# Edge net of a graph kernel: a visit's mask by six comparisons of a row with a column each

## The chip, the cores and the metric

One NeuronCore of a Trainium2 chip. The metric is the time of one execution on the device in microseconds, the median of three. A profile is one further execution, taken by the hardware profiler.

## The reference

6250 nodes with 64 features and 200,000 edges with a source and a destination (sorted by destination, denser towards low nodes) go through four layers of a graph network; each is preceded by a layer norm and a relu, and its result is added to `x`. The change lies in the last layer:

```python
src, dst = (edge_index[0], edge_index[1])
x = jnp.concatenate([node_features[src], node_features[dst], edge_features], axis=-1)
h = jax.nn.relu(x @ W1.T + b1)
messages = h @ W2.T + b2
agg = jax.ops.segment_sum(messages, dst, num_segments=node_features.shape[0])
...
return (1.0 - z) * n + z * node_features
```

## The kernel before

The three other layers multiply by a dense matrix of edge counts and are not touched. The last layer has a relu per edge, so it must go over every edge; this stage is called the edge net.

Edges lie in chunks of 128, one edge on each partition; six chunks are a group (GC = 6), 261 groups in all. Nodes lie in 49 tiles of 128. Since edges are sorted, a group holds edges of one tile or of neighbouring ones. A *visit* is a pair of group and tile; there are 309 (NV). Low tiles have many groups, high ones few, so that towards the end about three groups make four visits.

**GpSimd** fetches the source side. For each group it issues six indirect gathers (L704, one per chunk), each from `ptable` in DRAM (a row of 64 fp32 per node) into a slot of `grow`, a ring of eight groups in SBUF. The addresses are a column of `src_i` in SBUF. It does nothing else here. **SyncE** (`group`, L563 its wait) hands the slots on: it waits until the visits of the group four before are done, frees a slot, waits until the rows of this group have landed and counts up `s_land`, on which VectorE waits.

**ScalarE** issues two plain transfers per visit (`edge_rows`): the low bits of the destinations, broadcast to all partitions (`dst_rows`), and the edge features. It also computes the relu (L907).

**TensorE**, for a visit: `new(t, m)` makes the destination side with a one-hot matrix (L959) and adds the edge features' product (L962), into PSUM, two visits ahead. `seg(m)` (L970) sums messages by node: six matmuls, chunk j's mask as weights, against the three bf16 parts of its messages.

**VectorE**, for a visit, in program order (`visit`, one loop body unrolled for four visits, at whose head it loads the registers of the four; `m` is the slot of four):
- it waits for TensorE (`s_z`) and for the gathered rows (`s_land`)
- L1383: adds part 0 in PSUM to the gathered rows, 384 elements per partition
- L1346 `mask` of the next visit: 1 where edge and node of the tile agree, 128 x 6 elements
- L1383: adds part 1
- L1350 `relative`: six destinations less the tile's first node, for the visit after next
- L1383: adds part 2; ScalarE's relu starts
- L1357 `turned`: the one-hot matrix of the visit after next, by one comparison of 768 bf16 elements with a column
- it waits for the relu; L1406: its residual after one bf16 part; L1362: sums TensorE's result of two visits before; L1412: the second residual; L1367: adds the sum into `pair`.

The mask before compares `drel`, six int16 numbers per partition, each broadcast over 128 nodes, with `itiles`, a constant table of node numbers in [node][chunk] order. So a visit's masks are stored with the chunk innermost, and the weights of one chunk are read with a stride of six elements.

Of the kernel before, what the change touches and what calls it, by code (L numbers as in the profile page):

```python
# [22 lines left out]
P = 128  # L23
N = 6250
E = 200000
H = 64
# [9 lines left out]
GC = 6  # L36
# [5 lines left out]
DEEP = 4  # L42
# [37 lines left out]
bf16 = mybir.dt.bfloat16  # L80
# [5 lines left out]
ALU = mybir.AluOpType  # L86
ACT = mybir.ActivationFunctionType
AX = mybir.AxisListType.X
ds = bass.ds


def gnn(nc, D, out):
    with ExitStack() as ctx:
        def sb(name, shape, dt=f32):
            return ctx.enter_context(nc.sbuf_tensor(name, shape, dt))
# [46 lines left out]
        dst_s = sb("dst_s", [P, CHP], i16)  # L142
# [9 lines left out]
        iota_h = sb("iota_h", [P, WC], f16)  # L152
# [3 lines left out]
        tbase = sb("tbase", [P, NTP])  # L156
# [15 lines left out]
        stat_w = sb("stat_w", [P, 2 * NW])  # L172
# [12 lines left out]
        idx_at = itile_at + P // 2  # L185
# [7 lines left out]
        itiles = sb("itiles", [P, P, SC], i16)  # L193
# [52 lines left out]
        def late_part(width):  # L246
            lp[0] += width
            assert lp[0] <= 2 * CHP
            return late[:, lp[0] - width:lp[0]]
# [24 lines left out]
        def net_part():  # L274
            net_used[0] += DEEP * GC * P // 2
            assert net_used[0] <= TC
            return arena[:, net_used[0] - DEEP * GC * P // 2:net_used[0]]

        masks = net_part().bitcast(bf16).rearrange("p (q d j) -> p q d j", q=DEEP, j=GC)
        onehotT = net_part().bitcast(bf16).rearrange("p (q e) -> p q e", q=DEEP)  # L280
        dst_rows = net_part().bitcast(bf16).rearrange("p (q e) -> p q e", q=DEEP)
        e32t = net_part()[0:2 * F32, :].rearrange("p (q e) -> p q e", q=DEEP)
        drel = sb("drel", [P, 4, GC], i16)
        gath_w = late_part(GC * 3 * H // 2)
        gath = parts3(gath_w)
        qblk = gath_w[:, 0:TB * H].rearrange("p (n f) -> p n f", f=H)
# [631 lines left out]
        def _(pe):  # L918
# [33 lines left out]
            def edge_net():  # L952

                def new(t, m):
                    z = (ps_front, ps_back)[m % 2]
                    pe.wait_ge(s_ohT, 1)
                    pe.sem_inc(s_ohT, -1)  # L957
                    for j in range(GC):
                        pe.matmul(z[:, j // 2, j % 2 * 3 * H:(j % 2 + 1) * 3 * H], onehotT[:, m, j * P:(j + 1) * P],  # L959
                                  qsp[:, ds(t, 1), :], start=j % 2 == 0, stop=False)  # L960
                    for b in range(TH):
                        last = pe.matmul(edge_z[m % 2][:, b, :, 0, :], e32t[:, m, b * P:(b + 1) * P],  # L962
                                         W["w_e3"][:, :].rearrange("p (c f) -> p c f", f=H), start=False, stop=True)
                    last.then_inc(s_z, 1)

                def seg(m):
                    pe.wait_ge(s_rl, 1)
                    pe.sem_inc(s_rl, -1)  # L968
                    for j in range(GC):
                        last = pe.matmul(ps_d[:, m % 2, 0:3 * H], masks[:, m, :, j], msg_h[:, m, j, :, :],  # L970
                                         start=j == 0, stop=j == GC - 1)
                    last.then_inc(s_sg, 1)

                def visit(n, m, t):
                    if n is None or n + 2 < NV:
                        new(t, (m + 2) % DEEP)
                    seg(m)

                new(0, 0)
                t1 = pe.value_load(visit_tab[0:1, 0:1, 3, 3:4].rearrange("o b w -> o (b w)"), min_val=0, max_val=NT - 1)  # L980
                new(t1, 1)
                all_visits(pe, 2, 3, visit)
# [289 lines left out]
        def _(v):  # L1272
            def link(ins):

                ins.then_inc(s_v, 1)
                v.wait_ge(s_v, 1)
                v.sem_inc(s_v, -1)
# [65 lines left out]
            def edge_net():  # L1343

                def mask(m, n2):
                    return v.tensor_tensor(masks[:, m, :, :], drel[:, n2, :].unsqueeze(1).broadcast_to([P, P, GC]),  # L1346
                                           itiles[:, :, :], ALU.is_equal)

                def relative(c, t, n2):
                    return v.tensor_scalar(drel[:, n2, :], dst_s[:, ds(c, GC)], tbase[:, ds(t, 1)], None, ALU.subtract)  # L1350

                def turned(m):
                    v.wait_ge(s_db[m], 16)
                    v.sem_inc(s_db[m], -16)
                    v.wait_ge(s_et[m], 16)
                    v.sem_inc(s_et[m], -16)
                    v.tensor_scalar(onehotT[:, m, :], dst_rows[:, m, :], pcol[:, 0:1], None, ALU.is_equal).then_inc(s_ohT, 1)  # L1357

                def summed(m):
                    v.wait_ge(s_sg, 1)  # L1360
                    v.sem_inc(s_sg, -1)
                    return v.tensor_reduce(red[:, m % 2, :], ps_d[:, m % 2, 0:3 * H].rearrange("p (k f) -> p f k", k=3),  # L1362
                                           AX, ALU.add)

                def total(t, m):
                    sums = pair[:, ds(t, 1), 0:H].rearrange("p t f -> p (t f)")
                    return v.tensor_tensor(sums, sums, red[:, m % 2, :], ALU.add)  # L1367

                def visit(n, m, g1, c2, t2, before):

                    def has(k):
                        return n is None or 0 <= n + k < NV

                    q = nc.s_assert_within(v.snap((g1 + (RING - 1)) % RING), 0, RING - 1,
                                           skip_runtime_bounds_check_because="the remainder of a group's number")
                    v.wait_ge(s_z, 1)
                    v.sem_inc(s_z, -1)
                    v.wait_ge(s_land, v.snap(g1 & 511))
                    z = edge_z[m % 2]
                    sums = msg[:, m, :, 2, :].rearrange("p (b c) f -> p b c f", c=2)  # L1380

                    def add(k, other):
                        return v.tensor_tensor(sums, z[:, :, :, k, :], other, ALU.add)  # L1383

                    def linked(links):
                        v.wait_ge(s_v, links)
                        v.sem_inc(s_v, -links)

                    links = 1 if has(-3) else 0
                    add(0, grow[:, ds(q, 1), :, :].rearrange("p r (b c) f -> p (r b) c f", c=2)).then_inc(s_v, 1)  # L1390
                    if has(1):
                        mask((m + 1) % DEEP, (m + 1) % 2)
                    linked(1 + links)
                    add(1, sums).then_inc(s_v, 1)
                    links = 0
                    if has(2):
                        relative(c2, t2, m % 2).then_inc(s_v, 1)
                        links += 1
                    linked(1 + links)
                    add(2, sums).then_inc(s_y, 1)  # L1400
                    if has(2):
                        turned((m + 2) % DEEP)
                    v.wait_ge(s_r1, 1)
                    v.sem_inc(s_r1, -1)  # L1404
                    v.sem_inc(s_done, 1)
                    v.tensor_tensor(msg[:, m, :, 1, :], msg[:, m, :, 0, :], msg_h[:, m, :, 0, :], ALU.subtract).then_inc(s_v, 1)  # L1406
                    links = 1
                    if has(-2):
                        summed(m).then_inc(s_v, 1)
                        links += 1  # L1410
                    linked(links)
                    v.tensor_tensor(msg[:, m, :, 2, :], msg[:, m, :, 1, :], msg_h[:, m, :, 1, :], ALU.subtract).then_inc(s_rl, 1)  # L1412
                    if has(-2):
                        total(before, m).then_inc(s_v, 1)

                v.memset(pair[:, :, 0:H], 0.0)
                t1 = v.value_load(visit_tab[0:1, 0:1, 3, 3:4].rearrange("o b w -> o (b w)"), min_val=0, max_val=NT - 1)
                c1 = v.value_load(visit_tab[0:1, 0:1, 3, 0:1].rearrange("o b w -> o (b w)"), min_val=0, max_val=PAD_C)
                link(v.tensor_copy(drel[:, 0, :], dst_s[:, 0:GC]))
                mask(0, 0)  # L1420
                link(relative(c1, t1, 1))
                for m in range(2):
                    turned(m)
                all_visits(v, 0, 4, visit)
                v.wait_ge(s_v, 1)
                v.sem_inc(s_v, -1)
                for k in (NV - 2, NV - 1):
                    before = visits(v, (k + 2) // 4, 0, 4)[(k + 2) % 4][3]
                    link(summed(k))
                    link(total(before, k))  # L1430
# [608 lines left out]
```

## Time and profile before

| | |
|---|---|
| time, median of 3 | 4882.58 us (4882.41 to 4883.76) |
| the profiled execution | 4881.64 us, its span 4879.8 us |
| mean granted TensorE clock | 0.707 of full speed over the span, 0.50 in the edge net |
| edge net, from the first gather to the last sum | 2769.9 to 4787 us |
| busy over the span | TensorE 3312.7, VectorE 2846.7, ScalarE 886.2, GpSimd 2046.2 us |

Busy times of the span are averages over stages that have different limits; for the change, the edge net's own rows count. In them a start is in us from the span's start, the duration in us follows, and a bracket names what ended the idle time before.

### The profile page before, as it was taken

How to read it: one execution, taken by the hardware profiler on the slowest of the kernel's cores; microseconds unless marked ns; L12 is line 12 of the kernel's file. 1: busy time of each engine (PE TensorE's matmuls, PEld its weight loads, DVE VectorE, ACT ScalarE, POOL GpSimd, SP SyncE). 2: the span in 40 equal slices, each digit the busy share in tenths (PEclk: the TensorE clock that was granted, in tenths of full speed). 3: DMA queues.
4: the chain of work that ended last, by engine and by line, in shares of the span. 5: the costliest groups of instructions: out<-in, count | busy, mean ns of one | idle time of the engine just before them, and what ended most of it. 6: DMA issues, size and time to landing. Idle time of an engine off the chain costs nothing. (4 is left out here: it accounts for less than half of the span.)

```text
span 4879.8 us, 93316 instructions
## 1 busy us (share of the span) xinstructions
PE 3312.7 (68%) x24444; PEld 2509.9 (51%) x24445; DVE 2846.7 (58%) x7446; ACT 886.2 (18%) x1811; POOL 2046.2 (42%) x2644
## 2 busy tenths in 40 slices
PE   3332577787769899899989644555555556666666
PEld 2222233333349789798989533343444444444445
DVE  6667788777765534312323355555666666666775
ACT  1221123566630112100011100000000000000002
POOL 4666400000000211111111377777777777777770
PEclk6555899888889999999999655555555555555558
DMA  3000000111135234354544222222333233333330
GB/s 143 0 0 1 10 21 40 56 56 59 59 117 199 84 122 162 126 176 159 185 146 158 71 64 64 67 69 67 69 72 72 72 72 74 74 76 74 77 76 20
DMA packets 173539, 403.74 MB, mean 83 GB/s; under 512 B 47902, under 2 KB 109481, under 8 KB 172809
## 3 DMA queue, kind: packets, MB, share of 16 engines
q1 hardware_dynamic: 52409, 259.35, 14.9%
q10 hardware_dynamic: 69360, 91.59, 6.7%
q0 software_dynamic: 51680, 51.82, 6.0%
q8 instruction: 29, 0.48, 0.0%
q14 instruction: 61, 0.50, 0.0%
HBM read 359.52 MB, written 43.07 MB: 83 GB/s over the span
## 5 line engine op out<-in xcount | busy, mean ns | idle before, releaser
L704 POOL DMA_INDIRECT scr<-ptable,src_i x1566 | 1522.4, 972 | 481.5 <-issue 398.3
L673 POOL COPY late<-late 128x256 f32<-128x256 f32 (+1 forms) x65 | 25.9, 398 | 1950.8 <-POOLq L671 1950.8
L1037 PE MATMUL ps_front<-scr,arena 128*128 128x192 bf16 x7203 | 612.2, 248 | 66.7 <-PEq L1035 66.7
L1146 PE MATMUL ps_front<-stat_w,scr 128*128 128x392 fp8e4 x2064 | 492.7, 368 | 234.3 <-PEq L1150 206.9
L1037 PEld LDWEIGHTS ps_front<-scr,arena 128*128 128x128 fp8e4 x7203 | 601.2, 99 | 76.3 <-issue 74.5
L907 ACT ACTIVATE arena<-arena 128x384 f32<-128x384 f32 x309 | 161.6, 523 | 1859.6 <-ACTq L906 1859.6
L959 PE MATMUL ps_front<-arena 128*128 (+1 forms) x930 | 176.5, 362 | 436.0 <-PEq L957 436.0
L1658 DVE TENSOR_TENSOR scr<-scr,late 128x384 bf16<-128x384 f16 x1024 | 364.1, 356 | 183.6 <-DVEq L1657 175.7
L959 PE MATMUL ps_back<-arena 128*128 x924 | 175.4, 362 | 399.1 <-PEq L957 399.1
L1146 PEld LDWEIGHTS ps_front<-stat_w,scr 128*128 128x128 bf16 x2064 | 186.3, 104 | 503.5 <-issue 465.3
L1037 PE MATMUL ps_front<-arena 128*128 128x192 bf16 x4802 | 406.0, 248 | 23.4 <-PEq L1035 23.4
L1662 DVE TENSOR_TENSOR stat_w<-arena 128x294 int32 x904 | 416.4, 461 | 0.9 <-issue 0.7
L1037 PEld LDWEIGHTS ps_front<-arena 128*128 128x128 fp8e4 x4802 | 399.9, 98 | 27.4 <-issue 26.0
L1505 DVE TENSOR_REDUCE arena<-ps_front 128x64 f32<-128x192 f32 x196 | 70.1, 358 | 561.4 <-DVEq L1503 561.2
L959 PEld LDWEIGHTS ps_front<-arena 128*128 128x128 bf16 x930 | 113.5, 137 | 498.6 <-issue 492.7
L970 PE MATMUL ps_g<-arena 128*128 128x192 bf16 x1854 | 359.6, 362 | 8.9 <-PEq L968 8.9
L820 ACT ACTIVATE arena<-ps_front 128x392 fp8e4<-128x392 f32 x588 | 292.3, 497 | 328.0 <-ACTq L818 299.0
L959 PEld LDWEIGHTS ps_back<-arena 128*128 128x128 bf16 x924 | 112.9, 137 | 461.3 <-issue 455.5
L970 PEld LDWEIGHTS ps_g<-arena 128*128 128x128 bf16 x1854 | 233.4, 144 | 90.4 <-issue 78.3
L1406 DVE TENSOR_TENSOR arena<-arena 128x384 f32<-128x384 f32 x309 | 172.8, 559 | 168.0 <-DVEq L1404 168.0
L962 PE MATMUL ps_front<-sb_w_e,arena 64*128 64x128 f32 x930 | 255.3, 445 | 0.0
L962 PE MATMUL ps_back<-sb_w_e,arena 64*128 64x128 f32 x924 | 253.6, 445 | 0.0
(342 smaller groups left out, 4782.4 us busy)
## 6 DMA issues: line engine op xcount, KB each, us to landing
arena<-a_dram SPq DMA_DIRECT2D x245, 784.0 KB, 4.4
arena<-low_dram ACTq DMA_DIRECT2D x309, 192.0 KB, 3.3
a_dram<-arena SPq DMA_DIRECT2D x49, 784.0 KB, 3.3
arena<-in_e32g ACTq DMA_DIRECT2D x309, 96.0 KB, 3.2
scr<-ptable,src_i POOLq DMA_INDIRECT x1566
arena<-in_e16p SPq DMA_DIRECT2D x1, 13387.5 KB, 35.6
x<-in_x_nm SPq DMA_DIRECT2D x1, 1664.0 KB, 8.1
out_nm<-x SPq DMA_DIRECT2D x1, 1664.0 KB
```

The source lines that it names most:

```text
L704: pool.indirect_dma_start(grow[:, g % RING, j, :], None, ptable, bass.IndirectOffsetOnAxis(ap=src_i[:, g * GC + j:g * GC + j + 1], axis=0) ...
L820: act.activation(amat[b][:, :, w * DW:(w + 1) * DW], bank_w[w % GF][:, 0:WC].rearrange("p (s d) -> p s d", d=DW), ACT.Copy, scale=1.0 / SC ...
L907: act.activation(msg[:, m, :, 0, :], msg[:, m, :, 2, :], ACT.Relu).then_inc(s_r1, 1)
L959: pe.matmul(z[:, j // 2, j % 2 * 3 * H:(j % 2 + 1) * 3 * H], onehotT[:, m, j * P:(j + 1) * P], qsp[:, ds(t, 1), :], start=j % 2 == 0, stop ...
L962: last = pe.matmul(edge_z[m % 2][:, b, :, 0, :], e32t[:, m, b * P:(b + 1) * P], W["w_e3"][:, :].rearrange("p (c f) -> p c f", f=H), start= ...
L970: last = pe.matmul(ps_d[:, m % 2, 0:3 * H], masks[:, m, :, j], msg_h[:, m, j, :, :], start=j == 0, stop=j == GC - 1)
L1037: last = pe.matmul(ps_z[b % 2][:, 0:3 * H], amat[b][:, i, :], hsp[k % 2][:, i, :], start=(i == 0), stop=(i == NT - 1))
L1146: return pe.matmul(bank_w[i][:, 0:WC], oh_lo[u][:, j, :], oh_hi[u][:, j, :], **{"start": False, "stop": False, **flags})
L1406: v.tensor_tensor(msg[:, m, :, 1, :], msg[:, m, :, 0, :], msg_h[:, m, :, 0, :], ALU.subtract).then_inc(s_v, 1)
L1505: link(v.tensor_reduce(stage[:, j, 0:H], ps_z[j % 2][:, 0:3 * H].rearrange("p (k f) -> p f k", k=3), AX, ALU.add))
L1658: v.tensor_tensor(oh_lo[u].rearrange("p j (s a) -> p j s a", a=2), iota_w[:, k, :, :].unsqueeze(1).broadcast_to([P, GW, P // 2, 2]), keys[ ...
L1662: v.tensor_tensor(oh_hi_i[u], src_hot[:, ds(c, GW), :].unsqueeze(3).broadcast_to([P, GW, NT, 2]), dst_word[:, ds(c, GW), :].unsqueeze(2).b ...
```

## The change

The mask of a visit is made chunk by chunk. `mask` now issues six `tensor_scalar` comparisons: the row `iota_h[:, 0:128]` (f16) with one column of `erel` (fp32) each, into 128 neighbouring bf16 elements. `relative` writes `erel`, an fp32 place of two times six columns in `stat_w`, in place of the int16 `drel`. A visit's masks lie one behind the other, [chunk][node], and TensorE reads a chunk's weights contiguously. The visits, the waits, the transfers and the gathers are the same.

```diff
--- before.py
+++ after.py
@@ -276,11 +276,12 @@
             assert net_used[0] <= TC
             return arena[:, net_used[0] - DEEP * GC * P // 2:net_used[0]]
 
-        masks = net_part().bitcast(bf16).rearrange("p (q d j) -> p q d j", q=DEEP, j=GC)
+        masks = net_part().bitcast(bf16).rearrange("p (q j d) -> p q j d", q=DEEP, j=GC)
         onehotT = net_part().bitcast(bf16).rearrange("p (q e) -> p q e", q=DEEP)
         dst_rows = net_part().bitcast(bf16).rearrange("p (q e) -> p q e", q=DEEP)
         e32t = net_part()[0:2 * F32, :].rearrange("p (q e) -> p q e", q=DEEP)
         drel = sb("drel", [P, 4, GC], i16)
+        erel = stat_w[:, idx_at + GC:idx_at + 3 * GC].rearrange("p (b j) -> p b j", b=2)
         gath_w = late_part(GC * 3 * H // 2)
         gath = parts3(gath_w)
         qblk = gath_w[:, 0:TB * H].rearrange("p (n f) -> p n f", f=H)
@@ -967,7 +968,7 @@
                     pe.wait_ge(s_rl, 1)
                     pe.sem_inc(s_rl, -1)
                     for j in range(GC):
-                        last = pe.matmul(ps_d[:, m % 2, 0:3 * H], masks[:, m, :, j], msg_h[:, m, j, :, :],
+                        last = pe.matmul(ps_d[:, m % 2, 0:3 * H], masks[:, m, j, :], msg_h[:, m, j, :, :],
                                          start=j == 0, stop=j == GC - 1)
                     last.then_inc(s_sg, 1)
 
@@ -1343,11 +1344,11 @@
             def edge_net():
 
                 def mask(m, n2):
-                    return v.tensor_tensor(masks[:, m, :, :], drel[:, n2, :].unsqueeze(1).broadcast_to([P, P, GC]),
-                                           itiles[:, :, :], ALU.is_equal)
+                    for j in range(GC):
+                        v.tensor_scalar(masks[:, m, j, :], iota_h[:, 0:P], erel[:, n2, j:j + 1], None, ALU.is_equal)
 
                 def relative(c, t, n2):
-                    return v.tensor_scalar(drel[:, n2, :], dst_s[:, ds(c, GC)], tbase[:, ds(t, 1)], None, ALU.subtract)
+                    return v.tensor_scalar(erel[:, n2, :], dst_s[:, ds(c, GC)], tbase[:, ds(t, 1)], None, ALU.subtract)
 
                 def turned(m):
                     v.wait_ge(s_db[m], 16)
@@ -1416,7 +1417,7 @@
                 v.memset(pair[:, :, 0:H], 0.0)
                 t1 = v.value_load(visit_tab[0:1, 0:1, 3, 3:4].rearrange("o b w -> o (b w)"), min_val=0, max_val=NT - 1)
                 c1 = v.value_load(visit_tab[0:1, 0:1, 3, 0:1].rearrange("o b w -> o (b w)"), min_val=0, max_val=PAD_C)
-                link(v.tensor_copy(drel[:, 0, :], dst_s[:, 0:GC]))
+                link(v.tensor_copy(erel[:, 0, :], dst_s[:, 0:GC]))
                 mask(0, 0)
                 link(relative(c1, t1, 1))
                 for m in range(2):
```

## Rows read from the trace of the kernel before

**Rows 1.** Page, costliest groups: count | busy us, mean ns | idle before.

```profile
L704 POOL DMA_INDIRECT scr<-ptable,src_i x1566 | 1522.4, 972 | 481.5 <-issue 398.3
```

**Rows 2.** Timeline: first and last gather, first and last visit's first addition.

```profile
2769.91 0.99 POOL L704 DMA_INDIRECT scr<-ptable,src_i  x1 [4.59 <-POOLq L702]
...
2778.95 0.56 DVE L1383 TENSOR_TENSOR arena<-ps_front,scr 128x384 f32<-128x384 f32 x1 [9.93 <-SPq L563]
...
4768.07 1.15 POOL L704 DMA_INDIRECT scr<-ptable,src_i  x1 [0.30 <-issue]
...
4778.01 0.56 DVE L1383 TENSOR_TENSOR arena<-ps_front,scr 128x384 f32<-128x384 f32 x1 [0.98 <-DVEq L1377]
```

**Rows 3.** Waits in the edge net, VectorE: us in total, times, longest.

```profile
DVE arena L1383 <- SPq L563: 482.8, 200, 9.9
```

**Rows 4.** Timeline of a visit with a landing wait: start, duration, engine, line.

```profile
3207.39 0.95 POOL L704 DMA_INDIRECT scr<-ptable,src_i  x1 [0.30 <-issue]
3207.55 0.56 DVE L1383 TENSOR_TENSOR arena<-ps_front,scr 128x384 f32<-128x384 f32 x1 [2.41 <-SPq L563]
3208.03 0.55 DVE L1346 TENSOR_TENSOR arena<-drel,itiles 128x768 bf16<-128x768 int16 x1
3208.49 0.55 DVE L1383 TENSOR_TENSOR arena<-ps_front,arena 128x384 f32<-128x384 f32 x1
...
3209.81 0.41 DVE L1357 TENSOR_SCALAR arena<-arena,pcol 128x768 bf16<-128x768 bf16 x1
3209.90 1.14 POOL L704 DMA_INDIRECT scr<-ptable,src_i  x1 [0.30 <-issue]
...
3210.78 0.56 DVE L1406 TENSOR_TENSOR arena<-arena 128x384 f32<-128x384 f32 x1 [0.56 <-DVEq L1404]
...
3211.35 0.95 POOL L704 DMA_INDIRECT scr<-ptable,src_i  x1 [0.30 <-issue]
...
3211.76 0.56 DVE L1412 TENSOR_TENSOR arena<-arena 128x384 f32<-128x384 f32 x1
...
3212.60 0.95 POOL L704 DMA_INDIRECT scr<-ptable,src_i  x1 [0.30 <-issue]
...
3215.23 0.56 DVE L1383 TENSOR_TENSOR arena<-ps_back,scr 128x384 f32<-128x384 f32 x1 [2.78 <-SPq L563]
```

**Rows 5.** Timeline: a gather behind L1412, and one behind L1346.

```profile
3204.45 0.56 DVE L1412 TENSOR_TENSOR arena<-arena 128x384 f32<-128x384 f32 x1
3204.70 1.13 POOL L704 DMA_INDIRECT scr<-ptable,src_i  x1 [0.30 <-issue]
...
4755.86 0.55 DVE L1346 TENSOR_TENSOR arena<-drel,itiles 128x768 bf16<-128x768 int16 x1
4755.99 1.25 POOL L704 DMA_INDIRECT scr<-ptable,src_i  x1 [0.30 <-issue]
```

**Rows 6.** Timeline: L1357 begun late in a gather.

```profile
4743.36 0.95 POOL L704 DMA_INDIRECT scr<-ptable,src_i  x1 [0.30 <-issue]
...
4743.92 0.57 DVE L1357 TENSOR_SCALAR arena<-arena,pcol 128x768 bf16<-128x768 bf16 x1
```

**Rows 7.** Timeline of VectorE: short one-input instructions of several stages.

```profile
44.27 0.29 DVE L1771 TENSOR_SCALAR stat_w<-iota_h,vcol 128x316 bf16<-128x316 f16 x1
44.48 0.30 DVE L1772 TENSOR_SCALAR stat_w<-iota_h,vcol 128x316 bf16<-128x316 f16 x1
...
469.23 1.73 DVE L1859 TENSOR_SCALAR scr<-iota_h 128x128 f16<-128x128 f16 x16
...
2768.27 0.75 DVE L1357 TENSOR_SCALAR arena<-arena,pcol 128x768 bf16<-128x768 bf16 x2 [0.37 <-DVEq L1356]
```

**Rows 8.** Timeline: three visits' first additions, without a landing wait.

```profile
3273.80 0.55 DVE L1383 TENSOR_TENSOR arena<-ps_back,scr 128x384 f32<-128x384 f32 x1
...
3280.05 0.56 DVE L1383 TENSOR_TENSOR arena<-ps_front,scr 128x384 f32<-128x384 f32 x1 [1.36 <-DVEq L1377]
...
3284.86 0.55 DVE L1383 TENSOR_TENSOR arena<-ps_back,scr 128x384 f32<-128x384 f32 x1
```

## The prediction

> **What bounds the kernel now.** I read the page's costliest groups first. The largest is GpSimd's indirect gather, 1566 of them, 972 ns each [rows 1]. The timeline of the edge net then shows that they run without a pause: the first is issued at 2769.91 us, the last at 4768.07 [rows 2]. That is 1998.16 us for 1566 gathers, 1.276 us each, and 261 groups of six, so one group in 7.656 us. VectorE waits on the sync engine for rows that have not landed 200 times, 482.8 us [rows 3]; nothing makes GpSimd wait beyond its own 0.30 us between two gathers. So the stage lasts as long as the issue of the gathers, plus the last visits (the last begins 9.94 us after the last gather [rows 2]). Time saved or added on VectorE alone changes only its waits.
>
> But the gathers do not all take the same time. An undisturbed one takes 0.95 us and the next starts 1.256 us after it; the mean is 972 ns. The 22 ns over it, times 1566, are 34 us of the stage. Where they come from is in the timeline of one visit [rows 4]. Let its first addition (3207.55) be time 0. The gathers then start at -0.16, 2.35, 3.80 and 5.05 (one more, at 1.10, has no row here), and the one at 2.35 takes 1.14: VectorE's comparison L1357 had started 0.09 before it. The same happens with a gather that starts just after the mask of L1346 or the residual of L1412 began [rows 5]. With start plus overrun:
> - L1346 from 4755.86, gather 4755.99 longer by 0.30: released at +0.43.
> - L1412 from 3204.45, gather 3204.70 longer by 0.18: released at +0.43.
> - L1357 from 3209.81, gather 3209.90 longer by 0.19: released at +0.28.
> So each of these instructions shuts GpSimd out for a window: until 0.43 after its start for the mask and the two residual subtractions (768 two-byte or 384 four-byte elements), about 0.19 wide for L1357. The additions with one input in PSUM do nothing of the sort. Of the 230 gathers that overran by 0.02 or more, I laid each to the VectorE instruction that had just begun: L1357 13.2 us, L1406 6.7, L1412 6.6, L1346 6.3. It works the other way too: a one-input comparison that comes 0.56 after a gather's start takes 0.57 instead of 0.41 [rows 6], held until about 0.82 after the gather's start.
>
> That a DVE instruction with two SBUF inputs blocks GpSimd's reads, and a one-input one in a two-port mode blocks it altogether, is a rule of the Trainium skill (SBUF — State Buffer, Who interferes with whom), and by that rule the trace agrees. It also says that the holder keeps the ports for the whole instruction; the trace shows L1357 holding GpSimd for 0.19 us of its 0.41. If the six new ones held them throughout, it would be the third rival.
>
> **The change.** Removed: one L1346 per visit. It occupies VectorE from 8.03 to 8.49, 0.465 us [rows 4]. Added: six one-input comparisons of 128 elements with a column as operand. No such row is in the edge net; the nearest are these [rows 7]. Sixteen of the same size with a constant take 1.73 us, start to start 0.103. With a column as operand, 316 elements start 0.21 after each other; L1357, 768 elements, 0.34 start to start where two stand together. From these last two: (0.34-0.21)/(768-316) = 0.29 ns an element, and 0.12 to 0.13 fixed, so 0.162 for 128 elements. The floor is 0.103, the ceiling 0.21 (the 316 row itself). I take 0.162, for these have a column as operand. Six: 0.97 us (0.62 to 1.26), so VectorE's chain in a visit grows by 0.507 (0.16 to 0.80).
>
> The first of the six is also held once: it starts 0.48 into the visit, 0.64 after the gather at -0.16, and so waits for some 0.08. Everything behind it in the visit comes 0.59 later.
>
> Where that lies: a visit without a wait takes 4.81 (3181.99 to 3186.80 [rows 8]); one in four also has 1.44 for the registers of the next four. With 5.32 and a quarter of 1.44, 5.68, against an average of 1998/309 = 6.47 per visit from the gathers. Towards the end, where three groups make four visits, they allow 3 x 7.656/4 = 5.74: still above 5.68, though by little. So VectorE does not become the bound, and 0.507 x 309 = 157 us are hidden. What isn't hidden is the tail, three masks or so after the last gather: +2 us.
>
> The relative column: one L1350 either way, six elements, now written as fp32: nothing. TensorE reads its weights contiguously instead of with a stride of six; these matmuls lie beside VectorE's next visit (their sum is fetched two visits later), and the time between two visits covers them, so nothing, either way. No DMA, no wait and no queue is changed.
>
> **What it does to the gathers.** This is the sum. Windows that go: L1346's, 6.3 us. Windows that come: six of about 0.03 us, at most 0.03 each. Windows that move are what counts, because the visit starts a fixed 2.63 after its last gather (3212.60 to 3215.23 [rows 4]), so the same gather meets the same instruction visit after visit.
> - L1357 goes from 2.26 to 2.85: its window ends at 3.13 and begins near 2.95. The gather at 2.35 is past, that at 3.61 not yet there: free at the start, and its 13 us go.
> - L1406 from 3.23 to 3.82, window to 4.25: the gather at 3.61 has started, the next comes at 4.86. Free.
> - L1412 from 4.21 to 4.80, window to 5.23. The gather at 4.86 falls into it and is held until 5.23, by 0.37.
> That gather is the group's last, so the next visit starts at 5.23+2.63 = 7.86. Today the 120 long gaps between visits (over 7.3 us; first 2778.95, 7.57) have a mean of 7.643. +0.22 x 120 = +26 us.
> - Visits without a wait then start 5.32 apart. A gather that was released at the end of L1412's window has its fourth successor 5.02 later; the next window runs from 4.90 to 5.32 after it. It is held again, by 0.30. In the 95 short gaps the overruns are now 10.5 us, 0.11 each: +0.19 x 95 = +18 us. The 93 gaps between carry 2.5 us today: the extra 1.44 takes the gather out of step (fifth successor at 6.28, window from 6.34), 0.
>
> Sum: 26+18+2 = +46 us. On the profiled execution's 4881.64 (span 4879.8) that is 4927; it stands 0.9 below the median 4882.58, so I say **4927**. No change can be told within 0.2%, some 10 us.
>
> **Rivals.**
> - *Same time.* The step is less than I think. With a column operand as cheap as a constant (0.103) the shift is 0.16+0.08, L1412's window ends at 4.88, and the gather at 4.86 is hardly held; what was laid to L1346 and L1357 goes and L1406's (3.47 to 3.90, gather at 3.61) comes. About 4885. It decides where the shift is below 0.25. For it: gains and losses of windows roughly cancel if the gathers were spread evenly. Against: two rows with columns say 0.16. Chance 0.2. The Trainium skill (VectorE: DVE Perf Modes, The TRN2 errata) gives 58 cycles plus a quarter of the elements, an estimate of 94 ns for each of the six, 0.56 in all, and the same page warns that many small instructions pay the fixed part each time. By that figure it would be this rival; the rows with a column are above it.
> - *Faster.* The shift is over 0.66 (0.175 each and more). Then the gather at 4.86 starts before L1412's window opens, and nothing holds any gather of a steady visit: of their 20.1 us of overruns nearly all go, and the short visits stay as they are. -20+2: 4864. For it: only 0.015 us per comparison are missing. Against: at that length the later visits come close to the gathers' pace, and the landing itself scatters by 0.1, so some gathers are still caught. Chance 0.12.
> - *Much slower.* The six behave as one window, GpSimd not let in between them: from 0.57 to about 1.5. The gather at 1.10 waits 0.4 in each long gap, and every visit carries a window of 0.9 instead of 0.4: (0.9^2-0.4^2)/(2 x 1.256) = 0.26 x 309 = +80 us: 4963. Against: L1357's window is shorter than its duration. Chance 0.08.
>
> **How the numbers follow.** Forecast 0.6, the rivals 0.2, 0.12 and 0.08. The forecast's own range is 4905 (a shift of 0.45, where the hold shrinks) to 4945 (each caught for the full 0.42). Over all, 4884 to 4948 leaves out the faster and the much slower case. Faster 0.12, the same 0.2, slower 0.68.
>
> **What would show it.** Six comparisons 0.16 apart, the visit without a wait at 5.3; the mean gather at 1000 ns instead of 972, with the overruns at the start of L1412 and hardly any at L1357; 7.86 between steady visits. Wrong if the six stand 0.10 or 0.18 apart, if L1357, which begins its access 0.03 before GpSimd's own (2.95 against 2.35+0.62), stretches that gather or is pushed on together with L1406, or if a shut-out GpSimd makes up the time.

## The result, and the profile after

The changed kernel takes 4893.97 us (median of 16 runs, 4892.08 to 4898.34), the kernel before 4883.99 beside it. The ratio is 1.0022, 95% interval 1.0015 to 1.0030: slower by some 10 us, where 4927 was forecast. The sign was right and so was the instruction that holds the gathers; the size was over four times too large (46 us against 10). Four of the experiments below ran first on a chip on which every kernel, the kernel before too, took some 5550 us, and then once more (`_b`): both ratios are given, and the readings are of the second.

The page of the changed kernel, GpSimd's gathers among the costliest groups:

```profile
L705 POOL DMA_INDIRECT scr<-ptable,src_i x1566 | 1531.7, 978 | 481.7 <-issue 398.3
```

The gathers' busy time goes from 1522.4 [rows 1] to 1531.7 us, with the same 1566 of them, and the first and the last (2769.98 and 4777.43) lie 2007.45 apart instead of 1998.16 [rows 2]. That is 9.3 of the 11.4 us between the two profiled executions (4893.06 against 4881.64). The rest is behind the last gather, in the timeline of the stage's end: the last visit begins 12.38 instead of 9.94 us after it.

```profile
4777.43 1.23 POOL L705 DMA_INDIRECT scr<-ptable,src_i  x1 [0.30 <-issue]
...
4789.81 0.56 DVE L1384 TENSOR_TENSOR arena<-ps_front,scr 128x384 f32<-128x384 f32 x1 [1.37 <-DVEq L1378]
```

VectorE's waits for rows in the edge net, us in total, times, longest:

```profile
DVE arena L1384 <- SPq L564: 306.9, 154, 9.4
```

482.8 us [rows 3] became 306.9: 176 us of waiting were used up, against 157 worked out for the longer chain. VectorE's added work is hidden, as a total. (Idle time before the first addition that is laid to the loading of registers also rose, from 18.7 to 56.3 us.)

The timeline of one visit of the changed kernel, in which VectorE had waited for its rows:

```profile
2964.25 0.95 POOL L705 DMA_INDIRECT scr<-ptable,src_i  x1 [0.30 <-issue]
2964.43 0.56 DVE L1384 TENSOR_TENSOR arena<-ps_front,scr 128x384 f32<-128x384 f32 x1 [2.43 <-SPq L564]
2964.91 1.06 DVE L1348 TENSOR_SCALAR arena<-iota_h,stat_w 128x128 bf16<-128x128 f16 x6
...
2965.88 0.55 DVE L1384 TENSOR_TENSOR arena<-ps_front,arena 128x384 f32<-128x384 f32 x1
...
2966.77 0.95 POOL L705 DMA_INDIRECT scr<-ptable,src_i  x1 [0.30 <-issue]
2967.18 0.41 DVE L1358 TENSOR_SCALAR arena<-arena,pcol 128x768 bf16<-128x768 bf16 x1
...
2967.54 0.34 ACTq L900 DMA_DIRECT2D arena<-low_dram  x1
...
2968.02 0.95 POOL L705 DMA_INDIRECT scr<-ptable,src_i  x1 [0.30 <-issue]
...
2968.16 0.56 DVE L1407 TENSOR_TENSOR arena<-arena 128x384 f32<-128x384 f32 x1 [0.56 <-DVEq L1405]
...
2969.13 0.56 DVE L1413 TENSOR_TENSOR arena<-arena 128x384 f32<-128x384 f32 x1
2969.27 1.24 POOL L705 DMA_INDIRECT scr<-ptable,src_i  x1 [0.30 <-issue]
...
2972.26 0.56 DVE L1384 TENSOR_TENSOR arena<-ps_back,scr 128x384 f32<-128x384 f32 x1 [2.43 <-SPq L564]
```

With 2964.43 as time 0: the six comparisons start at 0.48 and the next addition at 1.45, so they take 0.97. L1407 starts at 3.73 (3.23 in [rows 4]), L1413 at 4.70 (4.21 there). The gather at 2.34 runs its 0.95 undisturbed, since L1358 comes 0.41 behind its start; the gather at 4.84 overruns by 0.29, held until 5.13, which is 0.43 after L1413 began. The next visit begins at 7.83, where it began at 7.68.

The overrun of a gather is its duration less 0.95 us. I laid each overrun of 0.02 us or more to the VectorE instruction that had begun last before the gather, as for the kernel before (there L1357 has 0.1 us more than in the prediction's count):

| overruns, us (times) | before | changed |
|---|---|---|
| mask (L1346 / six L1348) | 6.3 (32) | 1.1 (27) |
| one-hot (L1357 / L1358) | 13.3 (94) | 4.7 (57) |
| first residual (L1406 / L1407) | 6.7 (67) | 5.0 (36) |
| second residual (L1412 / L1413) | 6.6 (36) | 31.5 (128) |
| all | 33.0 | 42.3 |

### The profile page after: what moved, and what is told of

It is laid out like the page before. It is cut to its first block and busy times, and to the rows that moved or that the text cites. A ratio compares the mean times of both kernels' runs of the same rounds, so it can differ in the third digit from the quotient of the medians.

```text
span 4891.3 us, 94861 instructions
## 1 busy us (share of the span) xinstructions
PE 3307.2 (68%) x24444; PEld 2499.4 (51%) x24445; DVE 2994.3 (61%) x8991; ACT 886.5 (18%) x1811; POOL 2058.2 (42%) x2644
## 5 line engine op out<-in xcount | busy, mean ns | idle before, releaser
L705 POOL DMA_INDIRECT scr<-ptable,src_i x1566 | 1531.7, 978 | 481.7 <-issue 398.3
L1038 PEld LDWEIGHTS ps_front<-arena 128*128 128x128 fp8e4 x4802 | 399.9, 98 | 27.5 <-issue 26.1
L1348 DVE TENSOR_SCALAR arena<-iota_h,stat_w 128x128 bf16<-128x128 f16 x1854 | 337.8, 274 | 0.2 <-DVEq L1278 0.2
L1407 DVE TENSOR_TENSOR arena<-arena 128x384 f32<-128x384 f32 x309 | 172.6, 559 | 170.2 <-DVEq L1405 170.2
L971 PEld LDWEIGHTS ps_g<-arena 128*128 128x128 bf16 x1854 | 221.6, 135 | 95.0 <-issue 77.6
```

The lines of the kernel that those rows point to most:

```text
L705: pool.indirect_dma_start(grow[:, g % RING, j, :], None, ptable, bass.IndirectOffsetOnAxis(ap=src_i[:, g * GC + j:g * GC + j + 1], axis=0) ...
L971: last = pe.matmul(ps_d[:, m % 2, 0:3 * H], masks[:, m, j, :], msg_h[:, m, j, :, :], start=j == 0, stop=j == GC - 1)
L1038: last = pe.matmul(ps_z[b % 2][:, 0:3 * H], amat[b][:, i, :], hsp[k % 2][:, i, :], start=(i == 0), stop=(i == NT - 1))
L1348: v.tensor_scalar(masks[:, m, j, :], iota_h[:, 0:P], erel[:, n2, j:j + 1], None, ALU.is_equal)
```

## The experiments

Theory A: the time follows the sum of the gathers' overruns, which depends on where in a visit VectorE's windows stand (a window is the stretch of an instruction in which it holds back a gather that starts). Theory B: a longer chain on VectorE (the time from one visit's first addition to the next one's where nothing is waited for, its most frequent value) costs by its length. C: the six comparisons have a cost of their own. D: the layout helps TensorE. A *locked* visit is one that waited for its rows and begins less than 2.8 us after its group's last gather (after the gather's start plus its overrun; 2.64 is usual). The edits leave the waits between engines as they are; where the relative column is moved, VectorE's own wait for it moves along, to the second residual. An idle comparison is

```python
v.tensor_scalar(spare[k], iota_h[:, 0:P], pcol[:, 0:1], None, ALU.is_equal)
```

into a spare row that nothing reads.

**The shift alone, without the change: `before_pad3`.**

```diff
 mask((m + 1) % DEEP, (m + 1) % 2)
+for k in range(3):
+    v.tensor_scalar(spare[k], iota_h[:, 0:P], pcol[:, 0:1], None, ALU.is_equal)
```

> The kernel before, mask unchanged, with three idle comparisons of 128 elements behind the mask of every visit, 3 x 0.162 = 0.486 us; no result changes. Theory A (phase): everything behind the mask stands where it does in the changed kernel, within 0.02; L1412's overruns about 32 us, gap between locked visits 7.77, last gather near 2007 us after the first, time 4894 within 4 (the mask's own window stays, up to 6 us more). Theory C (the six comparisons' own windows or their layout cost the 10 us): at most half of it shows, 4884 to 4888.

Measured: 4913.84 us, ratio 1.0062 (1.0048 to 1.0076). The timeline of a locked visit:

```profile
2924.38 0.56 DVE L1384 TENSOR_TENSOR arena<-ps_back,scr 128x384 f32<-128x384 f32 x1 [2.44 <-SPq L564]
2924.86 0.55 DVE L1347 TENSOR_TENSOR arena<-drel,itiles 128x768 bf16<-128x768 int16 x1
2925.32 0.57 DVE L1395 TENSOR_SCALAR stat_w<-iota_h,pcol 128x128 bf16<-128x128 f16 x3
...
2928.09 0.56 DVE L1409 TENSOR_TENSOR arena<-arena 128x384 f32<-128x384 f32 x1 [0.56 <-DVEq L1407]
...
2929.07 0.56 DVE L1415 TENSOR_TENSOR arena<-arena 128x384 f32<-128x384 f32 x1
2929.22 1.23 POOL L705 DMA_INDIRECT scr<-ptable,src_i  x1 [0.31 <-issue]
...
2932.26 0.56 DVE L1384 TENSOR_TENSOR arena<-ps_front,scr 128x384 f32<-128x384 f32 x1 [2.50 <-SPq L564]
```

L1409 and L1415 stand at 3.71 and 4.69, where the change puts them; the gather at 4.84 is held by 0.28. L1415 has 41.5 us of overruns. But the old mask, still there, has 17.9 us in place of 6.3 (by what path was not looked into), and the time is 20 us above the 4894 that A gave, 14 above it with the 6 us allowed for the mask. So the shift alone costs 30 us. The changed kernel, with the same shift, takes 20 us less than this one: its overruns are 16.8 us less at the mask and 10.0 less at the second residual, and 5.7 more at the one-hot and the first residual. C falls (at most 4888 by it, and the six have 1.1 us of overruns between them), and B has no place for a kernel 20 us slower with the same chain (5.30 us, and 5.31 in the changed kernel).

**Half shifts: `before_pad1` and `before_pad2`.** One and two idle comparisons.

> The kernel before with one idle comparison of 128 elements (0.16 us) behind the mask of every visit. Theory A (phase): in a locked visit L1357 now begins at 2.42, behind the gather at 2.36, and its 13 us of overruns nearly go; L1406 runs from 3.39 with its window to 3.82 and holds the gather at 3.61 by about 0.22. Overrun of a locked visit 0.22 instead of 0.14, gap 7.73, time about 4895. Theory B (length of the chain, 30 us for 0.49): 4893, with the overruns still at L1412, not at L1406.

> The same with two (0.32 us). Theory A: L1406 starts at 3.55, its window 3.58 to 3.98 takes in the gather at 3.61 and holds it by up to 0.37, the largest of all; L1412 is free. Overruns at L1406 over 35 us, gap between locked visits about 7.85, time 4915 to 4925, slower than with three (4914). Theory B: 4903, between one and three.

Measured the first time: ratios 1.0031 (1.0020 to 1.0042) and 1.0086 (1.0068 to 1.0104). The second time:

> The kernel before with one idle comparison (0.16 us) behind the mask once more, on an undisturbed chip. Theory A: L1357's 13 us of overruns nearly go, L1406 holds the gather at 3.61 by about 0.22, gap between locked visits 7.73, time about 4895. Theory B: 4893 with the overruns still at L1412.

> The kernel before with two idle comparisons (0.32 us) behind the mask once more, on an undisturbed chip. Theory A: L1406's window 3.58 to 3.98 takes in the gather at 3.61; overruns at L1406 over 35 us, gap between locked visits about 7.85, 4915 to 4925, slower than with three (4914). Theory B: 4903.

Measured: 4898.57, ratio 1.0028 (1.0016 to 1.0040), and 4913.19, ratio 1.0059 (1.0042 to 1.0076). With one, L1358's overruns fell to 1.6 us as expected, but L1409 had only 9.3 and L1415 31.2, where B's text had them and not A's. With two, the 35 us expected at L1409 were 2.6, and L1415 had 51.3, in 242 visits. The timeline of a visit with two:

```profile
3005.23 0.56 DVE L1384 TENSOR_TENSOR arena<-ps_back,scr 128x384 f32<-128x384 f32 x1 [2.50 <-SPq L564]
...
3008.75 0.95 POOL L705 DMA_INDIRECT scr<-ptable,src_i  x1 [0.30 <-issue]
3008.83 0.56 DVE L1409 TENSOR_TENSOR arena<-arena 128x384 f32<-128x384 f32 x1 [0.56 <-DVEq L1407]
...
3009.80 0.56 DVE L1415 TENSOR_TENSOR arena<-arena 128x384 f32<-128x384 f32 x1
3010.01 1.18 POOL L705 DMA_INDIRECT scr<-ptable,src_i  x1 [0.30 <-issue]
```

L1409 starts at 3.60, 0.08 behind a gather (3.52) and not 0.03 ahead of one, so it holds nothing; the next gather comes 1.26 later, 0.21 into L1415, and overruns by 0.23. The time follows the overruns' total, as A says, but which instruction would hold was named wrongly: its place hung on 0.1 us. Two and three idle comparisons cost the same (4913.19 and 4913.84), where A had two slower than three and B had 4903 for two. Up to two, these times rise by 15 us for each idle comparison, as a theory of length would have it; what speaks against B are the third one and the runs below.

**More work on top of the change: `after_pad1`.** A seventh, idle comparison.

> The changed kernel with a seventh, idle comparison of 128 elements behind the six of every visit (it writes a spare row, no result changes), so VectorE works 0.16 us more per visit. Theory A (what costs is where VectorE's windows meet the gathers): the second residual L1413 now starts 4.87 after a visit's start instead of 4.71, behind the gather at 4.86 that it held by 0.28. Its share of the overruns falls from 31.5 us to under 12 us, the gap between locked visits from 7.79 to about 7.55, and the time is below the changed kernel's 4894: about 4878, although there is more work. Theory B (a longer chain on VectorE costs by its length, as +0.507 us per visit cost 10 us): another 0.16 costs 3 us or more, 4897 and up. Theory C (each small comparison costs its own window): 4896.

Measured: 4889.84, ratio 1.0012 (1.0003 to 1.0021): 4 us below the changed kernel, with more work. The timeline in a locked visit:

```profile
2936.01 0.95 POOL L706 DMA_INDIRECT scr<-ptable,src_i  x1 [0.30 <-issue]
2936.12 0.56 DVE L1416 TENSOR_TENSOR arena<-arena 128x384 f32<-128x384 f32 x1
```

L1416 begins 0.11 behind the gather and does not hold it. Its overruns fell from 31.5 to 23.2 us, all of them from 42.3 to 30.4. B and C, by which it would take 4896 or more, fall. The time expected, 4878, was missed by 12 us: L1416 kept twice the overruns expected, and the timeline of the end shows some 9 us more, for the last visit begins 21.85 us after the last gather (12.38 in the changed kernel).

```profile
4765.57 0.95 POOL L706 DMA_INDIRECT scr<-ptable,src_i  x1 [0.30 <-issue]
...
4787.42 0.56 DVE L1385 TENSOR_TENSOR arena<-ps_front,scr 128x384 f32<-128x384 f32 x1 [0.99 <-DVEq L1379]
```

The chain of a visit without a wait was now 5.48, with the quarter of 1.44 5.84 us, more than the 5.65 that three groups of undisturbed gathers (3 x 7.54) give each of four visits: towards the end VectorE sets the pace.

**The layout alone: `layout`.**

`by_chunk` is the masks' own place, read in [chunk][node] order.

```diff
-last = pe.matmul(ps_d[:, m % 2, 0:3 * H], masks[:, m, :, j], msg_h[:, m, j, :, :],
+last = pe.matmul(ps_d[:, m % 2, 0:3 * H], by_chunk[:, m, j, :], msg_h[:, m, j, :, :],
                  start=j == 0, stop=j == GC - 1)
```

> The kernel before, but TensorE reads the six masks of a visit as contiguous rows of 128 instead of with a stride of six; VectorE still stores them with the chunk innermost, so this leaves out the right sum by node. It times the layout alone. Theory A: nothing, 4883 within 2, weight loads 137 instead of 144 ns at most. Rival D (the layout gains some us on TensorE that the comparisons give back): 4878 or less.

Measured: 4883.93, ratio 1.0000 (0.9991 to 1.0009). The weight loads take 136 ns each instead of 144, and the time does not move. D falls.

**A window moved the wrong way, and then past: `before_rel` and `before_rel_pad`.**

```diff
-if has(2):
-    relative(c2, t2, m % 2).then_inc(s_v, 1)
-    links += 1
 linked(1 + links)
 add(2, sums).then_inc(s_y, 1)
 if has(2):
+    relative(c2, t2, m % 2).then_inc(s_v, 1)
     turned((m + 2) % DEEP)
...
-links = 1
+links = 2 if has(2) else 1
```

> The kernel before with the relative column (L1350) moved from between the second and third addition to behind the third, ahead of L1357. Same work and same results. The third addition then waits for the second alone and comes about 0.15 earlier, the relu and both residuals with it, while L1357 comes 0.07 later. Theory A: L1357's window (from 2.36) opens behind the gather at 2.36, L1406's closes at 3.51 ahead of the gather at 3.61, L1412's is 4.09 to 4.49 ahead of 4.86: hardly any overrun in locked visits, total overruns from 33 us to 15 or less, gap between locked visits 7.54 to 7.57, time 4866 within 6. Theory B (length of the chain alone): a visit without a wait 4.66 instead of 4.81 hides in the waits for rows, 4882.

Measured: 4903.02, ratio 1.0041 (1.0028 to 1.0055), slower where A expected 4866 and B 4882. The timeline:

```profile
2924.09 0.56 DVE L1383 TENSOR_TENSOR arena<-ps_back,scr 128x384 f32<-128x384 f32 x1 [2.98 <-SPq L563]
...
2926.20 0.23 DVE L1350 TENSOR_SCALAR drel<-dst_s,tbase 128x6 int16 x1
2926.34 0.41 DVE L1357 TENSOR_SCALAR arena<-arena,pcol 128x768 bf16<-128x768 bf16 x1
2926.41 1.16 POOL L704 DMA_INDIRECT scr<-ptable,src_i  x1 [0.30 <-issue]
```

L1357 starts 0.14 after the relative column there, where the column's duration of 0.23 had been reckoned, so it stands at 2.25 instead of 2.33 and still ahead of the gather at 2.32: 152 of them held, 24.3 us. The second residual, which A had free, has 14.3 us (6.6 before). This is read from the trace after the miss; the next run tests it by putting one idle comparison (0.16 us) between. Against B it speaks as it stands: the chain is shorter (4.67 instead of 4.81) and the kernel slower.

> The kernel before with the relative column behind the third addition, as in the run that moved it, and one idle comparison of 128 elements ahead of L1357. In that run L1357 began at 2.25 and held the gather at 2.32 to 2.36 in 152 visits, 24.3 us. Here it begins at 2.41. Theory A: L1357's overruns fall from 24 us to under 5, nothing takes their place in locked visits (residual windows 3.12 to 3.52 and 4.09 to 4.49), gap 7.55, time about 4882 against 4903 without the idle comparison. Theory B: the added comparison hides in VectorE's wait for the relu, 4903.

> The kernel before with the relative column behind the third addition and one idle comparison ahead of L1357, once more, on an undisturbed chip. Theory A: L1357's overruns fall from 24 us to under 5, gap between locked visits 7.55, time about 4882 against 4903 without the idle comparison. Theory B: 4903.

Measured: ratio 0.9993 (0.9980 to 1.0005) the first time, then 4886.28, ratio 1.0006 (0.9996 to 1.0015). The second one's timeline:

```profile
3001.68 0.25 DVE L1401 TENSOR_SCALAR stat_w<-iota_h,pcol 128x128 bf16<-128x128 f16 x1
...
3001.82 0.95 POOL L705 DMA_INDIRECT scr<-ptable,src_i  x1 [0.30 <-issue]
3001.84 0.41 DVE L1358 TENSOR_SCALAR arena<-arena,pcol 128x768 bf16<-128x768 bf16 x1
...
3002.53 0.56 DVE L1406 TENSOR_TENSOR arena<-arena 128x384 f32<-128x384 f32 x1 [0.27 <-DVEq L1404]
```

L1358 now starts 0.02 behind the gather, and no gather of this visit overruns. L1358 has 1.6 us in place of 24.3. An idle instruction in every visit took 17 us off the time. The long gaps have a mean of 7.53. Of what is left, 21.2 us are at the mask, nearly all in the three visits behind an edge between tiles.

**The comparisons where VectorE waits: `spread_cmp`.**

```diff
-if has(1):
-    mask((m + 1) % DEEP, (m + 1) % 2)
+if has(1):
+    mask((m + 1) % DEEP, (m + 1) % 2, (0,))
 linked(1 + links)
 add(1, sums).then_inc(s_v, 1)
-links = 0
+if has(1):
+    mask((m + 1) % DEEP, (m + 1) % 2, (1,))
+linked(1)
+add(2, sums).then_inc(s_y, 1)
 if has(2):
     relative(c2, t2, m % 2).then_inc(s_v, 1)
-    links += 1
-linked(1 + links)
-add(2, sums).then_inc(s_y, 1)
-if has(2):
     turned((m + 2) % DEEP)
+if has(1):
+    mask((m + 1) % DEEP, (m + 1) % 2, range(2, GC))
...
-links = 1
+links = 2 if has(2) else 1
```

> The changed kernel with its six comparisons put where VectorE waits anyway: the first between the first and second addition, the second between the second and third, the other four behind L1358, beside the relu; the relative column stands behind the third addition. Same work and results. The additions are then as close as their waits allow (0, 0.64, 1.27), the first residual at about 2.88 with its window to 3.31, the second at 3.86 with its window to 4.29. Theory A: gathers at 1.10, 2.36, 3.61, 4.86 miss all windows; total overruns from 42 us to 15 or less, gap between locked visits 7.54, a visit without a wait 4.5, time 4862 within 8, below both kernels. Theory B (length of the chain): it is back to below 4.81 and the time to 4883.

> The changed kernel with its comparisons spread over VectorE's waits (spread_cmp) once more: the four runs before this one fell on a chip on which every kernel, the kernel before too, took some 5550 us, with idle stretches of several us on all engines. Same expectation: additions at 0, 0.64, 1.27, first residual at about 2.88, second at 3.86, overruns 15 us or less, gap between locked visits 7.54, time 4862 within 8 by theory A, 4883 by theory B (length of the chain).

Measured: ratio 0.9971 (0.9961 to 0.9981) the first time, then 4875.23, ratio 0.9981 (0.9971 to 0.9991): faster than both kernels, by 9 us and 19 us, where A expected 4862 and B 4883. The timeline of a locked visit:

```profile
3012.72 0.56 DVE L1384 TENSOR_TENSOR arena<-ps_back,scr 128x384 f32<-128x384 f32 x1 [2.98 <-SPq L564]
3013.19 0.37 DVE L1348 TENSOR_SCALAR arena<-iota_h,stat_w 128x128 bf16<-128x128 f16 x1
3013.42 0.56 DVE L1384 TENSOR_TENSOR arena<-ps_back,arena 128x384 f32<-128x384 f32 x1
...
3013.90 0.25 DVE L1348 TENSOR_SCALAR arena<-iota_h,stat_w 128x128 bf16<-128x128 f16 x1
3014.13 0.56 DVE L1384 TENSOR_TENSOR arena<-ps_back,arena 128x384 f32<-128x384 f32 x1
...
3015.06 0.77 DVE L1348 TENSOR_SCALAR arena<-iota_h,stat_w 128x128 bf16<-128x128 f16 x4
3015.11 0.95 POOL L705 DMA_INDIRECT scr<-ptable,src_i  x1 [0.30 <-issue]
...
3015.74 0.55 DVE L1408 TENSOR_TENSOR arena<-arena 128x384 f32<-128x384 f32 x1
...
3016.70 0.56 DVE L1414 TENSOR_TENSOR arena<-arena 128x384 f32<-128x384 f32 x1
...
3020.32 0.56 DVE L1384 TENSOR_TENSOR arena<-ps_front,scr 128x384 f32<-128x384 f32 x1 [2.92 <-SPq L564]
```

The additions stand at 0, 0.70 and 1.41, L1408 at 3.02 and L1414 at 3.98, some 0.13 later than expected and still clear of the gathers. The gather at 2.39 starts beside the last four comparisons and takes its 0.95. The 120 visits that the next visit followed after more than 7.3 us in the kernel before (the long gaps) carry 2.2 us of overruns, 20.1 before. The others carry 24, nearly twice their 13: an order that suits one phase does not suit all.

**All together.** From each profiled execution (up to 3.2 us off the kernel's median): the time between the first and the last gather's start, and the execution's own time less that.

| kernel | overruns, us | first to last gather | rest |
|---|---|---|---|
| before | 33.0 | 1998.16 | 2883.5 |
| layout | 34.9 | 1999.82 | 2884.8 |
| changed | 42.3 | 2007.45 | 2885.6 |
| before_pad1_b | 47.9 | 2017.25 | 2883.4 |
| before_pad2_b | 62.0 | 2031.14 | 2885.0 |
| before_pad3 | 63.9 | 2030.83 | 2882.1 |
| before_rel | 52.1 | 2017.15 | 2883.9 |
| before_rel_pad_b | 37.1 | 2002.73 | 2885.6 |
| spread_cmp_b | 26.1 | 1996.15 | 2882.3 |
| after_pad1 | 30.4 | 1995.91 | 2894.2 |

Less its overruns, the second column is 1965 to 1970 us everywhere: 1565 x 1.256 = 1965.6 for undisturbed gathers, and overruns below 0.02, not counted. The rest is the same within 3.5 us, but for the one kernel in which VectorE took over. GpSimd waits 0.30 or 0.31 us between two gathers and never longer. So the difference in time between these kernels is that of their gathers' overruns, 26 to 64 us, and the pairs that differ in one small instruction or in the order alone (changed and after_pad1, before_rel and before_rel_pad_b, changed and spread_cmp_b) tie the overruns to what VectorE had just begun.

## Why the prediction was right in its sign and wrong in its size

- *What bounds the stage, and that 157 us of VectorE's work hide.* Right: 176 us of waits were used, the rest of the kernel is unchanged.
- *Six comparisons in 0.97 us, 0.162 each.* Right to 0.01 (0.48 to 1.45), and so was the price with a column as operand.
- *The first one held for 0.08 by GpSimd.* Wrong: the addition behind them started at 1.44 or 1.45 in 244 of 309 visits. The shift was 0.50, not 0.59, so L1413's window ended at 5.13 and not at 5.23. The held gather lost 0.25 in the mean of the locked visits instead of 0.37.
- *L1346's, L1357's windows go, L1412's comes.* Right: 6.3 to 1.1, 13.3 to 4.7, 6.6 to 31.5 us. By the rule of the Trainium skill (SBUF — State Buffer, Who interferes with whom) the holder keeps the ports for the whole instruction, and each of the six could have held a gather for all of its length; the trace has 27 holds of 0.04 us each, 1.1 us in all, so the measurement decides against it here.
- *The tail, +2.* Right, 2.4.
- *"the visit starts a fixed 2.63 after its last gather [...], so the same gather meets the same instruction visit after visit"*, for 120 long gaps, and held again in the 95 short ones. This is the step that failed: the terms +26 and +18. The 2.63 is not fixed. The first additions of five visits of the changed kernel around an edge between two tiles, in its timeline, with ScalarE's transfer and the last gather ahead of the fourth:

```profile
3071.08 0.55 DVE L1384 TENSOR_TENSOR arena<-ps_front,scr 128x384 f32<-128x384 f32 x1
...
3076.39 0.55 DVE L1384 TENSOR_TENSOR arena<-ps_back,scr 128x384 f32<-128x384 f32 x1
...
3083.28 0.56 DVE L1384 TENSOR_TENSOR arena<-ps_front,scr 128x384 f32<-128x384 f32 x1 [1.49 <-DVEq L1378]
...
3086.38 0.34 ACTq L900 DMA_DIRECT2D arena<-low_dram  x1
3086.55 0.95 POOL L705 DMA_INDIRECT scr<-ptable,src_i  x1 [0.30 <-issue]
...
3089.96 0.56 DVE L1384 TENSOR_TENSOR arena<-ps_back,scr 128x384 f32<-128x384 f32 x1 [1.29 <-SPq L564]
...
3097.26 0.56 DVE L1384 TENSOR_TENSOR arena<-ps_front,scr 128x384 f32<-128x384 f32 x1 [1.90 <-SPq L564]
```

Gaps of 5.31, 6.89, 6.68 and 7.30, then 7.42; the same visits of the kernel before have 4.81, 6.50, 6.67, 7.63 and 7.60. With 5.31 instead of 4.81 per visit VectorE comes out of an edge 0.5 us later for each visit without a wait, and takes more visits to be early again; meanwhile the gathers meet other instructions. The fourth visit did wait for its rows, and yet begins 3.41 after its group's last gather.

I counted, among the 120 (by their gap in the kernel before), those that are locked, that is, begin less than 2.8 us after the group's last gather. Before: 95, with 0.13 us of overruns each, and 25 others with 0.30. Changed: 53, with 0.25 each, and 67 others with 0.06. So 53 x 0.25 + 67 x 0.06 = 17 us, against 20.1 before: a loss of 26 us was a gain of 3. (The 53 have gaps of 7.80 in the mean, not 7.86; had all 120 been locked, the term would have been +18.) The short ones have 11.5 us (10.5 before; 28 expected). The gaps between, expected to be free, have 13.8 instead of 2.5, and that is the 10 us.

Of the 67, 64 had waited for their rows: VectorE was idle, and the rows came late. How late goes with ScalarE's two transfers (L900 is the first). From the group's last gather, counted as above, to the first addition, in the visits that waited for their rows:

| the first transfer was issued | before: visits, median, us | changed: visits, median, us |
|---|---|---|
| 1.75 us or more ahead of that gather | 121, 2.67 | 51, 2.66 |
| 1 to 1.75 us ahead | 45, 3.00 | 71, 2.93 |
| under 1 us ahead, or up to 1 us behind | 32, 3.71 | 30, 3.63 |

In the locked visit shown with the result it was issued at 2967.54, 1.73 ahead of the gather at 2969.27 and 2.02 ahead with its overrun; at the edge above at 3086.38, 0.17 ahead of it. The transfers follow the relu and so move with VectorE's visit, and a visit that is late against the gathers has its rows landing late, which keeps it late. The counts are shown; that the transfers delay the rows is argued from them, for no run moved the transfers alone.

I had worked out the phase of one steady visit and of a run of short ones, and applied them to all. The chain's length, which I had put under what hides, goes with how long the phase holds. Of the 120, the locked ones are 112 in spread_cmp_b (chain 4.57), 108 in before_rel (4.67), 95 before (4.81), 87, 76 and 71 with one to three idle comparisons (4.97, 5.14, 5.30), 53 in the changed kernel (5.31) and 19 in after_pad1 (5.48). It is not all: 71 and 53 have the same chain. Two slips of the working moved nothing: the 3181.99 and 3186.80 are not in [rows 8], which give the same 4.81, and 4881.64 + 46 is 4927.6.

What stays open: how the phases run across the edges of tiles was counted, not derived; nor did I test whether the same storage with one instruction per mask would do better.

## What to carry to other kernels

When GpSimd issues gathers back to back and sets the pace, what VectorE does beside it is not free even where it hides: here an instruction with two SBUF inputs lengthened a gather that started 0.04 to 0.40 us after it, and a one-input comparison of 768 elements one that started 0.08 to 0.26 us after it. Read the gathers' durations against what VectorE had just begun, sum the overruns, and judge an edit by that sum; a mean row does not show it. A time worked out for one steady iteration must be weighted by how many iterations are in that state after the edit, not before it.

## What the runs showed of the hardware

- Over the ten kernels of the table above the windows are sharp, as the delay of a gather against its start after that of the VectorE instruction. Mask (768 two-byte elements, two inputs): from 0.04 to 0.40, the overrun is 0.43 less the offset. The residuals (384 fp32, two inputs): the same. One-input comparison of 768: from 0.08 to 0.26, at most 0.21. Of 128, in the changed kernel: 27 times, 0.04 each. Additions with one input in PSUM: of 3296 gathers that started behind one, 33 overran, by 0.06 at most.
- The other way round, a one-input comparison of 768 elements that begins 0.49 to 0.71 after a gather's start takes from 0.64 down to some 0.44 instead of 0.41; begun up to 0.43, or 0.72 to 1.16 after it, it takes its 0.41.
- How long gathered rows take to land goes with how close ScalarE's plain transfers were issued: in the kernel before, a visit that waits for its rows begins 2.67 us after the last gather (median) with the transfers 1.75 us or more ahead of it, and 3.71 with them under 1 us ahead or up to 1 us behind. No run moved the transfers alone.
- An added idle instruction made a kernel faster twice: by 4 us (7 comparisons in place of 6) and by 17 us (4903 to 4886).
- Six comparisons of 128 elements with a column as operand take 0.97 us, 0.162 each. Sixteen instructions of 128 elements with a constant, an addition in another stage, start 0.103 after each other [rows 7]. That the column costs the 0.06 is likely and not shown: no run changes it alone.
